# A two-layer attention kernel on one core: every engine works on pairs of rows instead of single rows

## What is computed

```python
# layer 0, per row: layer norm, 8 heads of 32, a bias from x2d, a gate
x = _layernorm(x1d, norm_w, norm_b)
qkv = (x @ qkv_w.T).reshape(*x.shape[:-1], c, 3 * h)
aff = jnp.einsum('bmich,bmjch->bmijh', q, k)
gate = jax.nn.sigmoid(x @ gate_w.T + gate_b).reshape(*x.shape[:-1], c, h)
bias = x2d @ x2d_w.T * factor
weights = jax.nn.softmax(aff + bias[:, None], axis=-2)
out = jnp.einsum('bmrch,bmirh->bmich', v, weights) * gate
out = out.reshape(*x.shape[:-1], c * h) @ final_w.T + final_b
# layer 1, per row: 4 heads of 64, only |i - j| <= 16 kept
scores = jnp.where(jnp.abs(i - j) <= band, q @ k.T / sqrt(D) , -jnp.inf)
y = (softmax(scores) @ v) @ w_out.T + b_out
# around them
x = x + _L0_conv_ref(_gn(x), ...)
x = x + _L1_conv_ref(_gn(x), ...)
```

## Time and profile before

| | us |
|---|---|
| median of 3 runs | 3883.28 (3879.12 to 3885.64) |
| the profiled execution | 3882.37 |
| its span, first to last instruction | 3880.5 |
| PE busy | 3584.0 (92%) |
| DVE busy | 3097.5 (80%) |
| ACT busy | 2583.5 (67%) |
| POOL busy | 1994.2 (51%) |
| mean granted TensorE clock | 0.973 |

### The profile page before, as it was taken

How to read it: one execution, slowest core, us unless ns; L and a number is a source line. 1 busy time by engine, 2 the same in 40 slices (tenths; PEclk the granted TensorE clock), 3 DMA queues, 4 the chain that set the end, 5 groups by cost and what they waited for, 6 DMA issues and landing times.

```text
span 3880.5 us, 120998 instructions
## 1 busy us (share of the span) xinstructions
PE 3584.0 (92%) x36234; PEld 3025.6 (78%) x36234; DVE 3097.5 (80%) x11357; ACT 2583.5 (67%) x8615; POOL 1994.2 (51%) x3722
## 2 busy tenths in 40 slices
PE   4579999999999999999999997999999999999998
PEld 1167778778877787878877876888888888888887
DVE  4479999999999999999999996666667676666666
ACT  1158888888888888888888884555555555555554
POOL 0056666666666666666766663333333333333333
PEclk7589999999999999999999998999999999999999
DMA  9911111111111111111111110111111111111111
GB/s 366 350 44 50 48 42 49 49 49 42 47 49 49 46 43 49 49 49 41 49 49 49 45 44 31 44 43 49 43 49 43 49 43 49 43 49 45 47 47 41
DMA packets 189031, 238.40 MB, mean 61 GB/s; under 512 B 11824, under 2 KB 176176, under 8 KB 184752
## 3 DMA queue, kind: packets, MB, share of 16 engines
q1 hardware_dynamic: 184368, 204.17, 16.6%
q10 hardware_dynamic: 4608, 33.56, 2.3%
HBM read 170.57 MB, written 67.11 MB: 61 GB/s over the span
## 4 chain that ended last, share of the span: by engine, by line
PE 48%; DVE 18%; issue 13%; POOL 10%; ACT 5%; DMA 3%; DVEq 1%; ACTq 0%; POOLq 0%; SPq 0%
PE work L453 22%; PE work L462 5%; POOL prob L354 5%; PE turn L493 5%; PE turn L601 5%; PE mix L614 5%; ACT prob L686 4%; PE score L480 3%; DMA x_chunk<-xT 3%; PE score L584 3%; DVE att L999 2%; DVE kT L920 2%; POOL g_tok L368 2%; POOL g_tok L365 2%; DVE att L905 2%
## 5 line engine op out<-in xcount | busy, mean ns | idle before, releaser
L354 POOL TENSOR_SCALAR prob<-prob,row_inv 128x256 f32<-128x256 f32 x2048 | 1049.2, 530 | 681.0 <-DVE row_inv L874 668.4
L453 PE MATMUL work<-src,w 128*128 128x256 f32 x7680 | 1075.8, 289 | 40.1 <-DVE y_sb L856 29.9
L453 PEld LDWEIGHTS work<-src,w 128*128 128x128 f32 x7680 | 946.6, 189 | 161.8 <-issue 84.5
L686 ACT ACTIVATE prob<-prob,row_min 128x256 f32<-128x256 f32 x2048 | 1022.9, 504 | 38.9 <-DVE row_min L868 38.9
L868 DVE CUSTOM_DVE_ANT_0 prob<-score,neg_bias 128x256 f32<-128x256 f32 x2048 | 752.9, 419 | 112.2 <-PE score L480 101.5
L406 POOL TENSOR_SCALAR prob<-prob,row_inv 128x160 f32<-128x160 f32 x1024 | 387.8, 397 | 668.6 <-DVE row_inv L992 668.6
L748 ACT ACTIVATE prob<-prob,row_min 128x160 f32<-128x160 f32 x1024 | 426.5, 418 | 437.8 <-DVE row_min L971 437.8
L493 PE MATMUL turn<-ident,prob 128*128 128x128 f32 x4096 | 626.3, 275 | 35.4 <-DVE probT L879 29.9
L692 ACT COPY probT<-turn 128x512 f32<-128x512 f32 x512 | 299.4, 585 | 349.5 <-PE turn L493 349.5
L493 PEld LDWEIGHTS turn<-ident,prob 128*128 128x128 f32 x4096 | 462.7, 141 | 78.5 <-POOL prob L354 47.8
L453 PE MATMUL work<-att,wf 128*128 128x256 f32 x3072 | 433.4, 291 | 19.1 <-DVE att L999 2.3
(11 more groups left out here) (86 smaller groups left out, 5316.1 us busy)
## 6 DMA issues: line engine op xcount, KB each, us to landing
pair_chunk<-pairT ACTq DMA_DIRECT2D x32, 1024.0 KB, 7.5
x_chunk<-xT SPq DMA_DIRECT2D x32, 1024.0 KB, 8.0
x_sb<-xT SPq DMA_DIRECT2D x128, 256.0 KB, 3.4
x_tok<-x_nat SPq DMA_DIRECT2D x128, 256.0 KB, 3.4
x1T<-y_sb SPq DMA_DIRECT2D x128, 256.0 KB, 2.2
x_sb<-x1T SPq DMA_DIRECT2D x128, 256.0 KB, 2.9
outT<-y_sb SPq DMA_DIRECT2D x128, 256.0 KB, 2.2
prob<-w_d SPq DMA_DIRECT2D x1, 1024.0 KB, 8.4
```

Source lines behind the costliest of these rows:

```text
L354: pool.tensor_scalar(prob[:, h, ib], prob[:, h, ib], row_inv[:, h, ib:ib + 1], 1.0, ALU.mult, ALU.mult).then_inc(norm_done[0], 1)
L453: ins = pe.matmul(out[:, cb], w[:, of_w, kb, cols + cb * P:cols + (cb + 1) * P], x[:, of_x, kb], start=n == 0, stop=n == len(terms) - 1)
L686: act.activation(prob[:, h, ib], prob[:, h, ib], ACT.Exp, bias=row_min[:, h, ib:ib + 1], scale=-1.0, accum_out=row_sum[:, h, ib:ib + 1]).t ...
```

## The change

A unit of work is a pair of rows, 512 tokens; `over_pairs` runs 64 of them, four peeled at each end and the loop unrolled by two. Attention itself stays per row: a body has four quarters h = 0 to 3, with e = h // 2 the row of the pair, and h % 2 the half of the heads.

- `project` makes one channel block for 512 tokens: 6 matmuls of 512 instead of 12 of 256, into one whole bank (`A` or `B` of `work`). A pair takes 48 of these in stage 0 where 96 of 256 were, and 36 in stage 1 where 72 were. `project_tokens` stays at 256 columns, once for each row.
- ACT and DVE take q, k, gate, `xnT`, the residual and its sums per channel block of 512. ACT now writes both `xnT` and the high part of `src` from PSUM (`x_part`), in place of DVE's cast (L843).
- The group norm product and sum on POOL are one instruction each for 4 token blocks, the power and the variance once per pair. The product runs a pair ahead of the sum.
- `nqT` and `kT` have one buffer for a pair instead of two for rows; `att` and `gate` have two of a pair. `x_sb` and `y_sb` lie over the x2d chunks of the prologue, so SP waits for the last of these (`bias_ps`) ahead of the row loads; `x_chunk` lies over `probT`, `bias_rows` over `xnT`.
- In stage 1 x1 is loaded twice, into `x_ch` for the norm and into `x_sb` for the residual.

```diff
+PAIRS = ROWS // 2
+TOK2 = 2 * TOK
+PEEL = 4
+UNROLL = 2
...
+    with eng.bass.Fori(0, (PAIRS - 2 * PEEL) // UNROLL, engines=[eng.engine], hint_back_edge=True) as i:
...
+            def project(out, w, cols, x, cb):
+                terms = [(kb, part) for kb in range(CB) for part in PRODUCTS]
+                for n, (kb, (of_w, of_x)) in enumerate(terms):
+                    ins = pe.matmul(out, w[:, of_w, kb, cols + cb * P:cols + (cb + 1) * P], x[:, of_x, kb],
+                                    start=n == 0, stop=n == len(terms) - 1)
...
+                def untangle(out, cb):
+                    for tb in range(2 * TB):
+                        ins = pe.transpose(out[:, tb * P:(tb + 1) * P], xn[:, tb, cb * P:(cb + 1) * P], ident[:])
+                    ins.then_inc(t2_done, 1)
...
+                def x_part(cb, bank):
+                    wait(act, t2_done, nxt.times(CB, cb + 1))
+                    wait(act, src_done[0], nxt.times(CB, 0))
+                    wait(act, v_ps[0], p.times(2, 0))
+                    act.activation(xnT[:, cb], work[:, bank], ACT.Identity, scale=vec0_sb[:, 0, cb:cb + 1],
+                                   bias=vec0_sb[:, 1, cb:cb + 1]).then_inc(xnT_done, 1)
+                    act.activation(src[:, nxt.base % 2, HIGH, cb], work[:, bank], ACT.Identity, scale=vec0_sb[:, 0, cb:cb + 1],
+                                   bias=vec0_sb[:, 1, cb:cb + 1]).then_inc(src_high[0], 1)
...
+                def src_low(cb):
+                    wait(dve, src_high[0], nxt.times(CB, cb + 1))
+                    dve.tensor_tensor(src[:, nxt.base % 2, LOW, cb], xnT[:, cb], src[:, nxt.base % 2, HIGH, cb].bitcast(F32),
+                                      ALU.subtract).then_inc(src_done[0], 1)
...
-                for ob in range(CB):
-                    dve.scalar_tensor_tensor(out=y_sb[:, last.base % 2, ob], in0=work[:, bank, ob], scalar=bias[:, ob:ob + 1],
-                                             in1=x_sb[:, last.base % XSLOTS, ob], op0=ALU.add, op1=ALU.add
+                dve.scalar_tensor_tensor(out=y_sb[:, last.base % 2, ob], in0=work[:, 1 - ob], scalar=bias[:, ob:ob + 1],
+                                         in1=x_sb[:, last.base % 2, ob], op0=ALU.add, op1=ALU.add
```

More of the change, by code:

```diff
@@ L38 @@
 HPG = P // D0
-PAIRS0 = H0 // 2
 PAIR = 128
@@ new lines, in body0 @@
+                if last.exists:
+                    mixes(last, 3)
+                if p.exists:
+                    turns(0, 2)
+                    wait(pe, v_done[0], p.times(2, 1))
+                    project(B, w0, 3 * CH, x, 1).then_inc(gate_ps, 1)
+                    turns(0, 3)
+                    wait(pe, gate_done, p.times(HG, 1))
+                    project_tokens(A, w0, 2 * CH, x, 1).then_inc(v_ps[0], 1)
+                if p.exists:
+                    scores(p, 2)
+                    turns(1, 0)
@@ new lines, in body1 @@
+                if p.exists:
+                    turns(3, 0)
+                    mixes(p, 2)
+                if last.exists:
+                    if nxt.exists:
+                        wait(pe, q_done[1], nxt.times(CB, 2))
+                    elif p.exists:
+                        wait(pe, v_done[1], p.times(2, 2))
+                    else:
+                        wait(pe, y_done[1], last.times(CB, 0))
+                    project(A, wf1, 0, att[:, last.base % 2], 1).then_inc(y_ps[1], 1)
@@ L722, in body0 @@
-                if far.exists:
-                    wait(act, t2_done, far.times(1, 1))
-                    wait(act, src_done[0], far.times(1, 0))
-                    for cb in range(CB):
-                        act.activation(xnT[:, cb], work[:, 0, cb], ACT.Identity,
-                                       scale=vec0_sb[:, 0, cb:cb + 1], bias=vec0_sb[:, 1, cb:cb + 1]
-                                       ).then_inc(xnT_done, 1)
-                if m.exists:
-                    turn_copy(6)
@@ new lines, in body0 @@
+                if p.exists:
+                    inverse(p, 0, 1)
+                if nxt.exists:
+                    wait(dve, ln_rstd_done, nxt.times(1, 1))
+                    wait(dve, t2_done, nxt.times(CB, 0))
+                    normed(0)
+                    normed(1)
+                if p.exists:
+                    mins(p, 1, 0)
+                    mins(p, 1, 1)
+                    turn_copy(0, 1)
+                    mins(p, 1, 2)
+                    mins(p, 1, 3)
+                if last.exists:
+                    att_total(last, 1)
@@ new lines, in body0 @@
+                if p.exists:
+                    inverse(p, 1, 0)
+                    turn_copy(0, 3)
+                if last.exists:
+                    att_low(last, 1)
+                if nxt.exists:
+                    normed(2)
+                    normed(3)
+                if p.exists:
+                    inverse(p, 1, 1)
+                    mins(p, 2, 0)
+                    mins(p, 2, 1)
+                    turn_copy(1, 1)
+                if nxt.exists:
+                    src_low(0)
@@ L903, in body0 @@
+                if p.exists:
+                    mins(p, 2, 2)
+                    mins(p, 2, 3)
+                if nxt.exists:
+                    src_low(1)
+                if p.exists:
+                    inverse(p, 2, 0)
+                    turn_copy(1, 3)
                 if last.exists:
[L904 to L906 removed]
+                    residual(0, last, 0, vec0_sb[:, 3])
@@ L909, in body0 @@
                     apart(dve, dve_passed)
-                    for tb in range(TB):
+                    for tb in range(2 * TB):
                         dve.bn_stats(ln_st[:, tb], g_tok[:, far.base % 2, tb]).then_inc(ln_chain, 1)
-                    for tb in range(TB):
-                        wait(dve, ln_chain, far.times(2 * TB, tb + 1))
+                if p.exists:
+                    inverse(p, 2, 1)
+                    mins(p, 3, 0)
+                if last.exists:
+                    residual(0, last, 1, vec0_sb[:, 3])
@@ new lines, in body0 @@
+                if p.exists:
+                    mins(p, 3, 1)
+                    turn_copy(2, 1)
+                if nxt.exists:
+                    q_low(0)
+                if p.exists:
+                    mins(p, 3, 2)
+                    mins(p, 3, 3)
+                    att_total(p, 0)
+                    inverse(p, 3, 0)
+                    turn_copy(2, 3)
+                if nxt.exists:
+                    k_low(0)
+                if last.exists:
+                    out_stats(0)
```

1020 lines of the change are left out of this document (584 added, 436 removed).

## The result

| | us |
|---|---|
| before, median of 4 runs | 3884.46 (3879.12 to 3888.70) |
| after, median of 4 runs | 3933.33 (3931.29 to 3938.25) |
| ratio | 1.0128, 95% interval 1.0112 to 1.0144 |
| the profiled execution of after | 3935.06, its span 3933.2 |
| period of a pair in stage 0 | 34.68, before 33.60 |

The pair order is 1.3% slower, where 3820 us was forecast and 3890 us was the upper end of the range. The two profiled executions are 52.7 us apart. I place them by the periods: stage 0 loses 64 x 1.08 = 69 us, stage 1 gains 64 x 0.36 = 23 us, and +7 us is left for the edges.

What follows compares the result with a forecast made beforehand. PE and DVE in lockstep were taken to bound stage 0, PE alone stage 1. Stage 1 -50, stage 0 -23 and edges +10 make -63 us from 3882.4, forecast 3820 us, range 3715 to 3890.

Steps and rivals of the forecast that it cites:

- (a): Stage 0, PE's turns 0.2 waiting for DVE's copy of turns 0.1, behind POOL's power and normed: 1.6 us a pair.
- (b): Stage 0, PE's turns 1.3 waiting for ACT's copy of turns 1.2, behind two exps and two x_part: 1.6 us a pair.
- scores 0': Stage 0, PE's next scores 0 waiting for k_low 0, behind two mins, att_total and a copy: 0.45 us a pair.
- some 0.25 of shorter ones: Stage 0, PE's remaining short waits, not placed one by one: some 0.25 us of the 3.9 us a pair.
- projection term: PE's q, k and other wide projections: six 512-column matmuls at 1.39 us against twelve at 1.52, 0.13 us saved each.
- cold row: Projection matmuls at the 1.2 GHz clock: 0.229 us each against 0.213 of columns, read as 0.016 us fixed cost per instruction.
- list of PE's work in line: Stage 0, PE's steps of the new order laid end to end without any wait: 29.3 us a pair.
- Stage 1: Three wide projections save 0.39 us a row with no new wait: 10.99 us a row, 50 us less in all.
- Edges: Pipeline fill and bn_aggr: -3.6 us for bn_aggr, about +8 for stage 0, +6 for stage 1; sum +10 us.
- Rival 3: Width saves nothing, 0.254 us a matmul: stage 1 gains 0, stage 0 gains little, about 3880 us; chance 0.05.
- Rival 2: ACT's x_part ahead of copy 1.2 paces stage 0, from 34.3 us a pair on: slower, typically 3910 us; chance 0.14.
- forecast case: Stage 0 at 33.2 us a pair, PE's gain going almost wholly into waits: 3785 to 3855 us; chance 0.45.

Runs made afterwards that it cites:

- e6: The after kernel with ACT's x_part writing only xnT and DVE again casting the high part of src from it; 3891.95 us.
- e7: The after kernel with DVE's aggregates and variance right behind their statistics and POOL's power moved behind norms 2a; 3878.90 us.
- e12: The e3 kernel with POOL's group norm sum as four instructions of 256 columns instead of one of 1024; 3889.45 us.
- e3: The after kernel with DVE's normed 0 and 1, and their wait for POOL's power, moved behind its copy of turns 0.1; 3961.50 us.
- e1: The after kernel with each wide projection made of twelve 256-column matmuls instead of six of 512; 3945.56 us.
- e5: The after kernel with four streams of fp32r matmuls (128, 256 or 512 columns, new weight tile each) added on PE in the prologue; 3935.8 us, one run.

## Why the prediction was wrong

**The waits were right.** Forecast 3.9 us a pair. Measured in line: (a) 1.55 for 1.6, (b) 1.29 for 1.6, scores 0' 0.32 for 0.45 (0.17 of it the profile gives to issue, not to k), and 0.33 (`x_part 0`) and 0.39 (norms ahead of turns 0.0) for "some 0.25 of shorter ones". The sum is 3.88. The places, the releasers and the mechanisms were those named, and e6 and e7 each remove the one at which they aim. That ACT's instruction took 0.77 us and not 0.66 did not lengthen (b), since ACT came to it earlier than I had laid out. e12 and e3 show one thing that the layout lacked: which POOL instruction a DVE one meets.

**The projection term was not.** "0.13 us saved per projection" came to 0.03. The 0.233 us for a 512-column matmul was right (0.231). What was wrong is the other side of the subtraction: 0.127 for a 256-column one was a mean over a run, (1.68 - 0.28)/11, and held the 0.10 us that is lost once a run, spread over eleven steps. The repeated step is 0.118. Halving the number of matmuls doesn't halve a loss that comes once in either case. The cold row misled in the same way: 0.229 a matmul was read as 0.213 and 0.016 of fixed cost. Read one by one at the 1.2 GHz level, the starts are 0.213 apart with a first step of 0.38, and those of 512 columns 0.427 with a first of 0.59: there the repeated extra is zero. In stage 0 this term is 8 x 0.10 = 0.8 us a pair, 51 us in all.

**The list of PE's work in line was too short.** 29.3 us was put together from steps; measured it is 34.68 - 3.88 = 30.8. Of the 1.5 us, 0.8 are the projections above. 16 turns take 7.1 us and not 6.7: after scores they are 0.41 (1025.47 to 1025.88) or 0.49, not 0.36. The rest is 0.3 in small parts. The prediction had the means to see it: its own stall-free row of before is 15.6 us, 31.2 a pair, and less 8 x 0.13 that is 30.2, not 29.3. With the true 0.03 it is 31.0, and with the waits 34.9 against the measured 34.68. Part of this gap is the waits of before, which were taken from the list of waits and not in line. The other steps of the row show them:

```profile
1002.17 1.68 PE L453 MATMUL work<-src,w 128*128 128x256 f32 x12 [0.23 <-DVE y_sb L856]
...
1004.22 0.98 PE L480 MATMUL score<-kT,nqT 32*128 32x256 f32 x24
1005.48 0.63 PE L493 MATMUL turn<-ident,prob 128*128 128x128 f32 x4 [0.29 <-DVE probT L879]
...
1012.26 0.60 PE L493 MATMUL turn<-ident,prob 128*128 128x128 f32 x4
```

Turns to a projection took 0.83 us at 1001.34 where 0.35 is usual, turns to scores 1.03 at 1012.26 where 0.53 is, and scores to turns 1.26 at 1004.22 where 0.91 is: with 0.03 more at 1005.48 that is 1.36 us a row and not 1.16. PE's own work was thus 30.8 us a pair before, and by the same reading it is 30.8 after: what width saves, the other steps of the new order take back. A difference against a measured period needs only what changes; a list built anew must get every step right. So 0.7 us a pair, 45 us in all, is this error, and no experiment bears on it, only the accounting.

**Stage 1.** Forecast 22.0 us a pair, measured 22.40; -23 us for -50. No new wait came, as said (PE 1000 of 1000 us). Nearly all of the 0.36 gained is the wait for `att` that went (0.38, shown with the result), and not the width: e1, which undoes the width alone, gives back 0.09 of it (22.49 for 22.40), and about as much is lost again, as v takes 1.53 to 1.55 us instead of 1.48.

**Edges.** +7 for +10.

**The rivals.** Rival 3, that width saves nothing, was nearly right on the mechanism and had 0.05; its price of 3880 assumed that the period would not rise. With the forecast's own waits it would have been 34.24 us a pair, 64 x 0.68 = 44 us more in stage 0, and 3882 + 44 + 10 = 3936. That this is almost the measured 3933 is luck: stage 0 lost 28 us more than that, and stage 1 gained 23 where it has nothing. Rival 2 had the side and the deciding point: the pair took 34.68 us, over its 34.3. Its mechanism, ACT's chain, is only one half: e6 puts its worth at 41 us, e7 that of the power and the statistics at 54. Against the forecast case both were already inside the 3.9 us. What turned a gain of 23 us in stage 0 into a loss of 69 was the gain on PE that wasn't there: read in line, the waits rose from 2.7 us a pair to 3.9, and PE's own work stayed at 30.8 where a fall of 1.9 was booked.

The lower bound of that term was given as 0 in the prediction, and a pair then came to 33.2 + 1.04 = 34.2. The range didn't carry it through, as rival 3 let the waits absorb it; its upper end was too low by that reasoning, not by chance. Its 34.3 us, from which rival 2 should decide, is also 0.1 too high: 40 us over 64 pairs are 0.63, and 33.56 + 0.63 = 34.2.

## What to carry to other kernels

Read what one instruction costs from neighbouring starts, not from a mean over a run, when a change alters how many there are in a run: a loss that comes once hides in the mean. Cost an edit as a difference against the measured period, and if you also build the sum from steps, lay both next to each other; 0.9 us between them was the warning here. And when units of work are made twice as large, look at what stands ahead of each single-buffered hand-over: the wide steps (two normed, two `x_part`) stood in front of copies that PE needed at once, and moving the one and giving back the other was worth 94 us, twice what the pair order had lost. Last, look at more than one turn of the loop before you call an effect shown: e12 has two kinds of pair, 2.5 us apart, and one pair alone tells only one of them.

## What the hardware showed that was not expected

- The second matmul of a run of projections starts later than the spacing of the rest, by 0.10 us at the 2.4 GHz level and about 0.17 us at 1.2 GHz, at 256 and at 512 columns. Between e5's streams, where like follows like, it does not.
- With a new weight tile each time, matmuls of 128, 256 and 512 columns start 0.111, 0.120 and 0.229 us apart in e5, with ACT idle and POOL and DVE at work in part of the time. The Trainium skill, "TensorE: Matmul & The Clock Gate", section "Back-to-back issue gap", gives 131 ns at 512 columns for such a stream; e5 does not agree, and comes to nearly twice that.
- Two VectorE instructions from SBUF to SBUF take 0.73 us together with POOL idle and 0.96 to 1.07 beside its norms (after). Where they meet a GpSimd instruction of 2.4 us they take 2.9 to 3.4 us (e3), and where that is split in four, either 1.1 to 1.4 or 3.6 to 3.8 us (e12). VectorE is the one that stands: POOL's sum takes 2.42 us in the median where they meet and 2.36 where they do not.
- ScalarE's Identity with scale and bias from PSUM takes 0.77 us at 512 elements, 0.55 at 256.
- POOL's power takes 1.02 us for 128x4, against 0.70 for 128x2.
